# Selecting product keys as a pipeline over tiles with GpSimd's help, and a new order of two streams in a transformer kernel

## What is computed

```python
# norms of the decoder block
y = layernorm(y + sa, g1, beta1)
y = layernorm(y + ca, g2, beta2)
# differential attention: 16 heads a, mixed per row
att2 = att6[:, :, 0, :, 0, :] - lam * att6[:, :, 1, :, 1, :]
out = einsum('bnah,bhnd->bnad', att2, v)
out = out * rsqrt(mean(out * out, -1) + eps) * (1.0 - LAMBDA_INIT)
conn = x + out.reshape(b, n, d) @ Wo.T + bo
# feed-forward over product keys, 8 heads, 2 x 64 keys, top 16
sim = einsum('pbnhd,hkpd->pbnhk', q, keys)
sx, ix = top_k(sim[0], 16)
sy, iy = top_k(sim[1], 16)
all_scores = (sx[..., :, None] + sy[..., None, :]).reshape(b, n, 8, 256)
scores, pk_indices = top_k(all_scores, 16)
h = gelu(einsum('bnd,bnhkd->bnhk', x, W_down[pk_indices])) * softmax(scores)
x = x + einsum('bnhk,bnhkd->bnd', h, W_up[pk_indices])
```

## Time and profile before

| what | value |
|---|---|
| time, 3 runs | median 3420.44 us (3415.87 to 3421.91) |
| the profiled execution | 3419.78 us, span 3417.7 us |
| PE busy | 2563.9 us (75%) |
| PEld busy | 1837.5 us (54%) |
| DVE busy | 1929.2 us (56%) |
| ACT busy | 922.6 us (27%) |
| POOL busy | 667.3 us (20%) |
| mean granted clock of PE | 0.852 |

### The profile page before, as it was taken

The page is one execution under the profiler, slowest core; times in us unless marked ns, Lnnn a source line. Parts: engine busy times, 40 slices in busy tenths (PEclk is TensorE's granted clock), DMA queues, the critical chain, the costliest instruction groups (busy, mean ns, idle before and its releaser), DMA issues. The chain is left out here.

```text
span 3417.7 us, 47357 instructions
## 1 busy us (share of the span) xinstructions
PE 2563.9 (75%) x16384; PEld 1837.5 (54%) x16384; DVE 1929.2 (56%) x7470; ACT 922.6 (27%) x1994; POOL 667.3 (20%) x572
## 2 busy tenths in 40 slices
PE   5786888578984888858885789848888588866553
PEld 3584567345863557535674457635585356743331
DVE  2313455855747438564558556484385645683458
ACT  1212242123322233222421233212322224212210
POOL 0102114112221113021141122211130211411140
PEclk8698999789996899969997889969999799976666
DMA  6175144141623235141441416322251414412100
GB/s 233 44 249 191 38 159 156 64 165 59 202 105 112 87 94 200 68 155 38 150 165 64 163 55 193 120 102 98 85 209 67 150 44 144 171 64 101 25 0 7
DMA packets 215092, 392.59 MB, mean 115 GB/s; under 512 B 83728, under 2 KB 167952, under 8 KB 189616
## 3 DMA queue, kind: packets, MB, share of 16 engines
q1 hardware_dynamic: 208688, 372.49, 31.6%
q0 software_dynamic: 6144, 16.79, 1.5%
HBM read 350.55 MB, written 38.67 MB: 114 GB/s over the span
## 5 line engine op out<-in xcount | busy, mean ns | idle before, releaser
L799 PE MATMUL ps<-xbT,stream 128*128 128x128 f32 x2560 | 325.6, 283 | 12.8 <-DMA stream<-in_experts 8.4
L799 PEld LDWEIGHTS ps<-xbT,stream 128*128 128x128 f32 x2560 | 312.7, 198 | 25.1 <-DMA stream<-in_experts 13.2
L301 POOL TENSOR_TENSOR hTB<-pb,sbuf 128x2048 f32<-128x2048 f32 x32 | 152.0, 4763 | 431.4 <-DVE pb L1660 431.4
L1016 PE MATMUL ps<-ident,work 128*50 128x128 f32 x32 | 12.3, 385 | 240.5 <-DVE work L1799 240.5
L610 PE MATMUL ps<-cmat,aTB 128*128 128x512 f32 x256 | 144.3, 716 | 39.9 <-DVE sbuf L1744 36.2
L473 POOL TENSOR_TENSOR rstdB<-veB,mhalf 128x4 f32<-128x4 f32 x48 | 48.8, 1017 | 631.0 <-DVE veB L1281 631.0
L602 PE MATMUL ps<-ident,xnB 128*128 128x128 f32 x256 | 55.6, 338 | 154.1 <-DVE xnB L1288 122.8
L473 POOL TENSOR_TENSOR rstdA<-veA,mhalf 128x4 f32<-128x4 f32 x24 | 24.4, 1017 | 736.9 <-DVE veA L1281 736.9
L513 POOL DMA_INDIRECT hTA<-y_slots,slot x64 | 63.2, 988 | 518.6 <-DMA y_slots<-yb 501.5
L799 PE MATMUL ps<-xbT,ctxA 128*128 128x128 f32 x1280 | 158.2, 277 | 2.2 <-DMA ctxA<-in_experts 1.9
L799 PEld LDWEIGHTS ps<-xbT,ctxA 128*128 128x128 f32 x1280 | 150.8, 192 | 12.7 <-issue 5.2
(11 more groups left out here) (277 smaller groups left out, 5972.3 us busy)
## 6 DMA issues: line engine op xcount, KB each, us to landing
...
stream<-in_ctxT SPq DMA_DIRECT2D x16, 1024.0 KB, 10.7
```

Of the source, the lines that this page charges most:

```text
L301: return e.tensor_tensor(out.rearrange("p (a d h) -> p a d h", a=8, d=16), a.unsqueeze(2).broadcast_to([P, 8, 16, 16]), vals[:, t, :].rear ...
L799: ins = mm(ps[:, 2 * (b % 2) + u, f * P:(f + 1) * P], wu[:, u, k, f * P:(f + 1) * P], xbT[:, b % 2, k, :], start=k == 0, stop=k == KT - 1)
```

## The change

1. **Selection.** T + 2 steps of 6 slots in place of T + 1 of 7. In step i DVE does the first three operations of tile i, and the picks and shares of tile i-1. The candidate adds go from DVE to POOL, and so do the shares, the sum over heads (as 400, 200, 100 and 50 elements) and the product with the gelu values. `cand` and `s16` have two buffers. PE does the similarities of tile i+1 in slot c, as soon as tile i's banks are read, and the turn and the up product of tile i-2. The exponential (ACT) is one step later.
2. **Weighted values.** DVE's sums go to PSUM (`raw`), ACT squares them from there, and DVE scales from PSUM into `ob`. The scaling of tile i-2 stands ahead of the products of tile i.
3. **Norms y1 and y2.** The weight is multiplied in by POOL, ahead of its bias add.
4. **ORDER.** 131 back slots, and another interleaving. Expert block 0's up half is behind the third slot of the scores, no longer ahead of them. Expert block 11's up half and block 12's gate half are ahead of the second feed-forward, where blocks 10 and 11 stood. The gathers are in the selection's step 2 and the accumulations ahead of its last step; both stood behind the whole selection.

```diff
-    "bbbbfbfbbbfbfbbbfbfbffbfbffbfbbffbfbfbbbfbbfbbffbfbfbfbffbffbbbbfbfbfbfbbbbbfbffbffbbfbbfbfbbbfb"
...
+    "bbbbfbfbbbfbbfbbfbfbffbfbffbfbfbfbfbfbfbbfbbffbfbbfbfbffbbfbfbbbfbfbfbbfbbbbffbfbfbbbffbfbbfbbbf"
...
+        raw = ps[:, 6, :].rearrange("p (s n) -> p s n", s=2)
...
-        s16 = sbuf[:, 1024:1280].rearrange("p (a k) -> p a k", a=NPH)
-        cand = hTB[:, 0:8 * NP].rearrange("p (h n) -> p h n", h=8)
+        s16s = [a.rearrange("p (a k) -> p a k", a=NPH) for a in (sbuf[:, 1024:1280], hTB[:, 1536:1792])]
+        cands = [hTB[:, c:c + 8 * NP].rearrange("p (h n) -> p h n", h=8) for c in (0, 1024)]
...
-                        def with_bias(tag, be, dst):
+                        def with_bias(tag, gain, be, dst):
                             def then(slot):
                                 if slot == 1:
                                     for t in range(T):
-                                        pool.wait_ge(vec_done, V[tag, "g", t])
+                                        wait_scaled(pool, tag, t)
+                                        pool.wait_ge(pe_done, PE[tag, "T", t])
+                                        nc.gpsimd.tensor_tensor(dst[:, t], dst[:, t], w[gain], ALU.mult).then_inc(pool_done, O.step(tag, "g", t))
+                                    for t in range(T):
+                                        pool.wait_ge(pool_done, O[tag, "g", t])
                                         add(tag, t, dst[:, t], dst[:, t], w[be])
                             return then
...
+                        for i in range(T + 2):
+                            yield
+                            yield
+                            if i < T:
+                                t = i
+                                s16, cand = s16s[t % 2], cands[t % 2]
+                                pool.wait_ge(vec_done, V["picked", t])
+                                if t >= 2:
+                                    pool.wait_ge(vec_done, V["rep1", t - 2])
+                                sx, sy = s16[:, 0:8, :], s16[:, 8:16, :]
+                                off = 0
+                                for a0, a1 in ((0, 1), (1, 2), (2, 3), (3, 4), (4, 5), (5, 8), (8, 16)):
+                                    na, nb = a1 - a0, TOP // a1
+                                    c4 = cand[:, :, off:off + na * nb].rearrange("p h (a b) -> p h a b", a=na)
+                                    nc.gpsimd.tensor_tensor(c4, sx[:, :, a0:a1].unsqueeze(3).broadcast_to([P, 8, na, nb]),
+                                                            sy[:, :, 0:nb].unsqueeze(2).broadcast_to([P, 8, na, nb]),
+                                                            ALU.add).then_inc(pool_done, O.step("cand", t))
+                                    off += na * nb
+                                assert off == NP
+                            for _ in range(3):
+                                yield
+                            if 1 <= i <= T:
+                                t = i - 1
+                                pool.wait_ge(vec_done, V["ri", t])
+                                nc.gpsimd.tensor_tensor(cexp[:, t % 2], cexp[:, t % 2], b16(ri[:, 0, 0:8], NP),
+                                                        ALU.mult).then_inc(pool_done, O.step("shares", t))
+                                for half in (4, 2):
+                                    pool.wait_ge(pool_done, O.n)
+                                    nc.gpsimd.tensor_tensor(cexp[:, t % 2, 0:half], cexp[:, t % 2, 0:half], cexp[:, t % 2, half:2 * half],
+                                                            ALU.add).then_inc(pool_done, O.step())
+                                pool.wait_ge(pool_done, O.n)
+                                nc.gpsimd.tensor_tensor(phd[:, t % 2, :], cexp[:, t % 2, 0], cexp[:, t % 2, 1], ALU.add).then_inc(
+                                    pool_done, O.step())
+                                pool.wait_ge(pool_done, O.n)
+                                if t >= 2:
+                                    pool.wait_ge(pe_done, PE["uT", t - 2])
+                                pool.wait_ge(act_done, A["g50"])
+                                nc.gpsimd.tensor_tensor(u50[:, t % 2, :], phd[:, t % 2, :], g50[:, t * NP:(t + 1) * NP],
+                                                        ALU.mult).then_inc(pool_done, O.step("u50", t))
...
+                        for i in range(T + 2):
                             if i == 0:
                                 pe.wait_ge(vec_done, V["h2", "f2", T - 2])
                                 for t in range(T):
                                     ins = project(ps[:, 7, t * NP:(t + 1) * NP], aTB, t, kt("wd50"), slice(0, NP))
                                 ins.then_inc(pe_done, PE.step("h50"))
-                            if i >= 1:
-                                t = i - 1
-                                pe.wait_ge(vec_done, V["u50", t])
+                            yield
+                            yield
+                            if i + 1 < T:
+                                sim(i + 1)
...
+                            if 1 <= i <= T:
+                                t = i - 1
+                                act.wait_ge(vec_done, V["pred", t, 1])
+                                if t >= 2:
+                                    act.wait_ge(vec_done, V["rms", t - 2])
+                                sa(squares[:, t % 2, :], raw[:, t % 2, :], ACT.Square).then_inc(act_done, A.step("squares", t))
...
                         def output(t, j, products):
-                            vv.tensor_reduce(ob[:, t, j * 128:(j + 1) * 128], products.rearrange("p (n h) -> p n h", h=16),
+                            vv.tensor_reduce(raw[:, t % 2, j * 128:(j + 1) * 128], products.rearrange("p (n h) -> p n h", h=16),
                                              AX.X, ALU.add).then_inc(vec_done, V.step("pred", t, j))
 
                         def mean_squares(t):
-
-                            v.wait_ge(pool_done, O["pprod", t])
-                            output(t, 1, prodP[:, t % 2, :])
-                            own_steps()
-                            vv.tensor_tensor(squares[:, t % 2, :], ob[:, t, :], ob[:, t, :], ALU.mult).then_inc(vec_done, V.step())
-                            own_steps()
+                            v.wait_ge(act_done, A["squares", t])
                             vv.tensor_reduce(mx[:, t % 2, 0:16], squares[:, t % 2, :].rearrange("p (a d) -> p a d", a=16), AX.X,
                                              ALU.add).then_inc(vec_done, V.step())
                             own_steps()
-
                             vv.tensor_scalar(mx[:, t % 2, 16:32], mx[:, t % 2, 0:16], RMS / 16, EPS * RMS, ALU.mult,
                                              ALU.add).then_inc(vec_done, V.step("rms", t))
...
-                            if i < T:
-                                values(i)
-                            yield
                             if i >= 2:
                                 t = i - 2
                                 v.wait_ge(pool_done, O["rms", t])
-                                o3 = ob[:, t, :].rearrange("p (a d) -> p a d", a=16)
-                                vv.tensor_tensor(o3, o3, b16(mx[:, t % 2, 0:16], 16), ALU.mult).then_inc(vec_done, V.step("l4", "o", t))
+                                v.wait_ge(vec_done, V["pred", t, 1])
+                                vv.tensor_tensor(ob[:, t, :].rearrange("p (a d) -> p a d", a=16),
+                                                 raw[:, t % 2, :].rearrange("p (a d) -> p a d", a=16),
+                                                 b16(mx[:, t % 2, 0:16], 16), ALU.mult).then_inc(vec_done, V.step("l4", "o", t))
+                            if i < T:
+                                values(i)
+                            yield
+                            if 1 <= i <= T:
+                                v.wait_ge(pool_done, O["pprod", i - 1])
+                                output(i - 1, 1, prodP[:, (i - 1) % 2, :])
...
+                                    vv.max(s16[:, a, 8:16], rep64[:, a, :]).then_inc(
+                                        vec_done, V.step(*(("picked", t) if a == NPH - 1 else ())))
+                            yield
+                            if 1 <= i <= T:
                                 t = i - 1
-                                v.wait_ge(pe_done, PE["up", t])
-                                vv.tensor_tensor(xnB[:, t, :], ps[:, 7, 0:D], xB[:, t, :], ALU.add).then_inc(vec_done, V.step("x6", t))
...
+                                cand = cands[t % 2]
+                                v.wait_ge(pool_done, O["cand", t])
                                 own_steps()
                                 for h in range(8):
                                     vv.max(cm[:, h, :], cand[:, h, :]).then_inc(vec_done, V.step())
                                 own_steps()
+                                if t >= 2:
```

(8 more changed lines are left out.)

111 lines of the change are left out of this document (41 added, 70 removed).

## The result

The changed kernel takes 3386.46 us in the median of 4 runs (3377.23 to 3393.56), the kernel before, with one more run, 3418.15: a ratio of 0.9914, with a 95% interval of 0.989 to 0.9938. That is faster by 0.9%, 32 us. The forecast was 3382 us in a range of 3360 to 3410. The profiled execution is the slowest of the four, 3393.56 us with a span of 3391.8, so its span is 25.9 us under that of before.

What follows compares the result with a forecast made beforehand. No engine fills an iteration: VectorE nearly fills the selection, TensorE and VectorE the weighted values. Per iteration -0.2 - 6.1 - 0.4 + 1.0 + 0.4 = -5.3 us, seven times -37, last group -0.7: 3382 us, range 3360 to 3410.

Steps and rivals of the forecast that it cites:

- Selection, -6.1 us an iteration forecast: Selection: small operations moved to GpSimd and pipelined tiles give -7.9 us at best, less 1.8 for port waits.
- the head's wait for TensorE: Start of the selection: VectorE idles 2.5 us until tile 1's similarities are ready at 10.7 us.
- The term of the port: Selection: VectorE's subtraction and mask wait beside GpSimd's adds, 0.5 us for each of three tiles, plus 0.3 for the exponential.
- the prediction's sign that VectorE has no wait over 0.3 us after tile 1's max: Selection: after waiting 2 to 3 us for tile 1's max, VectorE was to run without longer waits.
- D: Selection: rival that the gathers hold up tile 2's candidates on GpSimd; 3413 to 3420 us, chance 0.08.
- B: Selection: rival that GpSimd bounds it and the kernel is slower; 3540 us at 1.5 us an operation, chance 0.08.
- The end of the iteration: After the last output add: accumulations (3.42 us) go in the chain's shadow; output issue 0.6 and landing 1.8 us remain.
- Weighted values, +1.35 and +1.0 us: Weighted values: +1.35 us as scaling waits for GpSimd's power, +1.0 for expert work that doesn't fit on TensorE.
- rival A: Weighted values: the block moved in finds no gap, the second feed-forward slips 4 us; 3403 us, chance 0.14.
- 1.5 was forecast for the scores' part: Ahead of the weighted values: their stage starts 1.5 us earlier as an expert up half leaves the place before the scores.
- The -0.4 at the key tile: First norm: weight products leave VectorE, four of them ahead of the first key tile, saving 0.4 us an iteration.
- Last group: Group after the loop, low clock: selection gains 2.0 us, weighted values lose 1.3, so -0.7 us.

Runs made afterwards that it cites:

- turn_first: Changed kernel with TensorE's turn and projection of a scaled tile one slot earlier and ScalarE's copy ahead of the next tile's square, in the weighted values: 3371.48 us.
- values_old: Changed kernel with the weighted values as before (sums into SBUF, square on VectorE, scaling behind the products): 3390.21 us, ratio 0.9925.
- order_only: Kernel before with only the new order up to the selection, old selection, values and norms: 3419.5 us, ratio 1.0013.
- sel_only: Kernel before with only the new selection; old values, norms and order up to the selection: 3388.06 us, ratio 0.992.
- block_out: Changed kernel with one expert block moved from the weighted values into the selection, tile 1's similarities first, gathers later: 3421.28 us, ratio 1.0024.

## Why the prediction was right

**Selection, -6.1 us an iteration forecast.** It was to be 69.3 us from first max to last add and is 70.64. GpSimd's prices held (2.1 and 3.0 forecast, 1.8 to 2.1 and 2.7 to 3.0 measured), and so did every position up to tile 1's picks, and the head's wait for TensorE (2.37 us, forecast 2.5). The term of the port was too large: subtractions took 0.68, 0.58, 0.68 and 0.92 us in place of 0.57, 0.6 a group and not 1.5. No mask was held (0.57 to 0.58), and in the iteration read here no operation of GpSimd ran beside one. The accumulations were held (4.47 against 3.38 us), in a place where it costs nothing. The prediction cites the Trainium skill, "SBUF — State Buffer", section "🔬 SBUF: two separate sides", by which the two exclude each other for a whole instruction. By that rule the trace agrees in kind: what is left of a GpSimd operation of 0.3 to 0.6 us is a short wait, and the add that meets a running subtraction takes 0.61 us in place of 0.28. What the sum had no term for is the standstill of about 2 us: without it the selection takes 68.5 (turn_first), 0.8 under the forecast. It also breaks the prediction's sign that VectorE has no wait over 0.3 us after tile 1's max. Candidates were never late, so D is out, and GpSimd is busy 25.7 of 70.6 us, so B is far off.

**The end of the iteration.** Forecast -2.3 us from last add to the next iteration (4.67 of work against 2.4 of issue and landing), measured 8.56 - 6.49 = 2.1.

**Weighted values, +1.35 and +1.0 us.** The stage grew by 2.44 us, and the sum of 2.35 met it by luck, since both terms were wrong. Beside the new order the new form costs nothing (changed 58.75 and 58.90, values_old 58.87), where 1.35 was forecast; the order alone costs 2.6 (order_only), where 1.0 was. The 1.35 is the price of a chain over VectorE, ScalarE and GpSimd, and in the new order that chain does not set the stage, TensorE's does. The last group has the new form and no expert work: there the stage is 0.6 us longer than before (55.13 to 55.77) and 0.4 longer than in values_old and sel_only (55.41). What the form costs in an iteration of the old order was not run. The wait that showed up when a block was taken out, ScalarE's turned copy behind its square (block_out), is not in the prediction, which had the power of GpSimd as the one that is late.

Of the signs, the stage by the prediction's own bounds, to the down product ahead of the feed-forward, went from 49.8 to 51.7 us, where 50 to 51 was expected. The second feed-forward starts 2.0 us later against the scores (88.90 to 90.92), and more than 1 us was to be the sign of rival A: TensorE did take back more than the sum had, at half the size that A gave it. Its slip of 4 us occurred in one iteration of seven of the profiled run (62.04 us for the stage, with 1.80 us of DMA wait for `xb` in it), not as the rule.

**Scores and norms.** The values start 1.1 us earlier relative to the first feed-forward (0.7 and 0.4 in the table); 1.5 was forecast for the scores' part. The -0.4 at the key tile shows as -0.1 to -0.3, and is not resolved: the same stretch runs from 94.6 to 96.5 us in the other kernels of the table.

**Last group.** Forecast -0.7, measured 332.8 to 333.0, +0.2. Its selection gained 3.6 us (71.32 to 67.70), more than the 2.0 forecast. The values gave 0.6 of it back, where 1.3 was forecast. The 1.4 us that the stretch from the first feed-forward to the scores lost there (73.38 to 74.76) are unexplained; sel_only has them too, so they come with part 1. The rest lies in the stretch ahead of it, which runs from 54.5 to 57.9 us over the traces.

**Sum.** Forecast -5.3 an iteration, the two traces -3.6: the standstill (2.2) less the port's overcharge (0.9) and some 0.4 of small terms. In the medians 32 us were gained where 38 were forecast. So the mechanism of the selection was right, and that the total came within 5 us of the forecast is in part luck: two misses of the selection have opposite signs.

**What stays open.** What brings VectorE's standstill. It moves with the gathers, and in each of the 42 iterations that have it (six traces) it ends 11.2 to 11.4 us behind the first gather, as the gathers' last packet starts at 11.2 to 11.3. Yet it disappears when only the slots of TensorE and ScalarE in another stage are moved (turn_first), which leaves VectorE's and GpSimd's programs as they are and the gathers' packets where they were. A late supply of instructions would fit the label "issue" but isn't shown: in the changed kernel no packet of an instruction queue falls between 5 and 15 us behind the first gather, and turn_first, without a standstill, has none between 5 and 13.
